# First-block scores of an attention kernel computed on array halves, with a rearranged opening

## The reference

```python
x = L0_attn_x                                  # (16, 256, 128), float32
xn = layernorm(x)
q = (xn @ Wq) ; k = (xn @ Wk)                  # 16 heads of 8
v = (xn @ Wv)                                  # 16 heads of 64
scores = einsum('bhqd,bhkd->bhqk', q, k) / sqrt(8)
scores = where(causal, -inf, scores)
ctx = einsum('bhqk,bhkd->bhqd', softmax(scores), v)
x = x + ctx.reshape(B, T, 1024) @ Wo
x = x + experts(layernorm(x), gate_w, w1, w2)  # softmax gate, top 64, gelu, scatter back
```

## Time and profile before

| | us |
|---|---|
| median of 3 runs (lowest to highest) | 560.72 (559.99 to 560.88) |
| the profiled execution | 560.4 |
| its span, first to last instruction | 558.7 |
| busy PE, DVE, ACT, POOL in that span | 527.9, 415.7, 403.8, 253.5 |

### The profile page before, as it was taken

How to read it: one execution, slowest core, us unless ns; L and a number is a source line. 1 busy time by engine, 2 the same in 40 slices (tenths; PEclk the granted TensorE clock), 3 DMA queues, 4 the chain that set the end, 5 groups by cost and what they waited for, 6 DMA issues and landing times.

```text
span 558.7 us, 13959 instructions
## 1 busy us (share of the span) xinstructions
PE 527.9 (94%) x4777; PEld 427.2 (76%) x4777; DVE 415.7 (74%) x1066; ACT 403.8 (72%) x1383; POOL 253.5 (45%) x249
## 2 busy tenths in 40 slices
PE   1389999999999999999999999999999999999996
PEld 1257777777777877877777777777789998999995
DVE  1477888888888888888898999899873776542354
ACT  4688888888888988989889888889745434334230
POOL 5165555555556556565565565556820101011011
PEclk9979999999999999999999999999999999999999
DMA  4585251732544225042250523410300011000011
GB/s 122 150 211 154 53 151 52 230 118 58 149 117 113 77 73 150 24 126 76 76 149 16 142 76 77 131 22 29 106 21 1 2 39 59 20 21 11 11 29 49
DMA packets 49783, 45.97 MB, mean 82 GB/s; under 512 B 4288, under 2 KB 46528, under 8 KB 49728
## 3 DMA queue, kind: packets, MB, share of 16 engines
q1 hardware_dynamic: 48864, 44.60, 29.2%
q10 hardware_dynamic: 864, 0.66, 0.4%
HBM read 26.35 MB, written 18.89 MB: 81 GB/s over the span
## 4 chain that ended last, share of the span: by engine, by line
PE 90%; ACT 4%; DVE 4%; issue 1%; DMA 1%; POOL 0%; ACTq 0%; DVEq 0%; POOLq 0%
PE ctx_ps L1075 16%; PE misc_ps L1084 12%; PE t_ps L1162 10%; PE t_ps L1048 6%; PE t_ps L1058 5%; PE t_ps L1049 5%; PE s_ps L1189 4%; PE misc_ps L1034 4%; PE s_ps L1146 4%; PE misc_ps L1036 3%; PE misc_ps L1035 3%; PE s_ps L1147 3%; PE s_ps L1148 3%; PE s_ps L1276 3%; PE ctx_ps L1172 2%; ACT prob L529 2%
## 5 line engine op out<-in xcount | busy, mean ns | idle before, releaser
L529 ACT ACTIVATE prob<-s_ps,neg_max 128x128 f32<-128x128 f32 (+1 forms) x512 | 209.9, 437 | 21.2 <-DVE neg_max L939 18.2
L489 POOL TENSOR_TENSOR probn<-prob,inv 128x1024 f32<-128x1024 f32 x64 | 121.2, 1893 | 56.3 <-DVE inv L960 56.3
L529 ACT ACTIVATION_READ_ACCUMULATOR prob<-s_ps,neg_max 128x1 f32 x512 | 114.5, 224 | 0.0
L482 POOL TENSOR_TENSOR probn<-prob,inv 128x512 f32<-128x512 f32 x64 | 66.5, 1040 | 77.7 <-PE t_ps L1058 69.6
L883 DVE TENSOR_REDUCE neg_max<-s_ps 128x4 f32<-128x1024 f32 x64 | 76.4, 1193 | 0.8 <-PE s_ps L1194 0.8
L1084 PE MATMUL misc_ps<-wo_sb,ctxT 128*128 128x128 f32 x512 | 73.9, 287 | 0.7 <-DVE x_all L708 0.7
L506 POOL TENSOR_TENSOR y_parts<-y_sb,y_parts 128x512 fp32r<-128x512 f32 x16 | 20.6, 1287 | 112.6 <-ACT y_parts L587 112.6
L1084 PEld LDWEIGHTS misc_ps<-wo_sb,ctxT 128*128 128x128 f32 x512 | 62.0, 191 | 11.4 <-issue 11.4
L577 ACT ACTIVATE hT<-s_ps 128x512 f32<-128x512 f32 x64 | 38.0, 597 | 44.7 <-PE s_ps L1148 42.2
L1048 PE MATMUL t_ps<-ident,probn 128*128 128x128 f32 x256 | 62.9, 285 | 0.5 <-ACT probT L543 0.5
L1049 PE MATMUL t_ps<-ident,probn 128*128 128x128 f32 x256 | 60.2, 275 | 0.0
(11 more groups left out here) (176 smaller groups left out, 1155.1 us busy)
## 6 DMA issues: line engine op xcount, KB each, us to landing
qT<-q_rows SPq DMA_DIRECT2D x15, 512.0 KB, 4.0
q_rows<-qk_hi SPq DMA_DIRECT2D x32, 128.0 KB, 2.4
q_rows<-qk_lo SPq DMA_DIRECT2D x32, 128.0 KB, 2.4
k_diag_odd<-k_rows SPq DMA_DIRECT2D x32, 128.0 KB, 4.2
k_rows<-qk_hi SPq DMA_DIRECT2D x30, 128.0 KB, 2.4
k_rows<-qk_lo SPq DMA_DIRECT2D x30, 128.0 KB, 2.4
k_diag_even<-k_rows SPq DMA_DIRECT2D x28, 128.0 KB, 4.2
w_raw<-in_L_ffn_w SPq DMA_DIRECT2D x1, 2048.0 KB, 9.5
```

The lines of the kernel that those rows point to most:

```text
L482: nc.gpsimd.tensor_tensor(probn[r][:, 0:HG * P].rearrange("p (i k) -> p i k", i=HG), prob[r][:, 0:HG * P].rearrange("p (i k) -> p i k", i=HG),
L489: nc.gpsimd.tensor_tensor(probn[r][:, HG * P:].rearrange("p (i k) -> p i k", i=HG), prob[r][:, HG * P:].rearrange("p (i k) -> p i k", i=HG ...
L529: last = nc.scalar.activation(prob[r][:, first + i * keys:first + (i + 1) * keys], scores[:, i, :], ACT.Exp, bias=neg_max[:, r, block_, i: ...
```

## The change

- First-block scores (`scores`) are two matmuls of 64 rows and 256 columns, `first_block(0)` on the lower and `first_block(1)` on the upper half of the array. Both write the one bank of `s0_ps`; a new semaphore `s0_half`, raised by `first_block(0)`, is waited for ahead of `first_block(1)`.
- First-block and second-block scores of a unit are issued together, at the end of slot u for unit u+2, in the order first(0), second(1), second(0), first(1), masks. The two halves of the array go through their two products in opposite orders. The wait for the exponentials of the unit before stands now between first(0) and second(1), ahead of `s0_done`.
- `turn(u-1)` comes first in PE's slot, ahead of queries and keys.
- DVE: the gate copy (L727) moves ahead of norms in slot 0; the second norm's statistics go behind the split of q and k in slot 3.
- Opening: the slots of b = -2 and -1 are replaced by a written-out sequence. DVE normalises batch 0 before it splits the weights of q and k. POOL makes both scales before the masks. Zeros of `k_diag` are made by ACT (two instructions) and DVE (six). ACT issues two of the first five loads. Second batch's norm, q and k, and values of units 0 and 1 come ahead of the scores of units 0 and 1.

The diff, cut to this:

```diff
@@ SP
                 if b < RING:
-                    sp.wait_ge(zeroed, b + 1)
+                    sp.wait_ge(zeroed, 3 + 4 * b)
                 if b == 0:
-                    load_rows(b, slice(0, 1), first_loaded)
+                    load_rows(b, slice(0, 1), first_loaded, range(2))
@@ POOL
+            norm1_scale(0)
+            norm1_scale(1)
+            masks()
...
@@ ACT
-            zero_keys(0)
...
+            split_norms(0, 0)
+            zero_keys(0, range(2))
+            split_qk(0)
+            act.wait_ge(qk_hi_done, 1)
+            store_rows(act, qk_hi, K_HI)
+            act.wait_ge(qk_lo_done, 1)
+            store_rows(act, qk_lo, K_LO)
+            act.wait_ge(wv_loaded, 16)
+            nc.scalar.activation(wv_hi[:, :], wv_raw[:, :], ACT.Copy).then_inc(w_hi, 1)
+            split_norms(1, 1)
+            act.wait_ge(qk_stored, QK_STORES)
+            act.wait_ge(zeroed, 3)
+            for i in range(2, HG):
+                act.dma_start(f32(k_diag[0][i * ROWS:(i + 1) * ROWS, 0:1, i, :]),
...
+            copy_values(0, 0, 0)
+            copy_values(1, 1, 0)
+            split_qk(1)
+            act.wait_ge(max0, 1)
+            exps(0, 0, s0_ps, P, 0, exp0)
+            act.wait_ge(max1, 1)
+            exps(0, 1, s1_ps, T, HG * P, exp1)
@@ DVE
+            norm_stats(lambda tb: x_all[:, tb, :], bn6, mv1, bn1_done, 1, stats1)
+            norm1(0)
+            split_qk_weights()
+            dve.wait_ge(x_loaded[1], 16)
+            norm_stats(lambda tb: x_all[:, TB + tb, :], bn6, mv1, bn1_done, 2, stats1)
+            split_norms(0, 0)
+            zero_keys(0, 2)
+            split_qk(0)
+            zero_keys(0, 3)
+            norm1(1)
+            zero_keys(1, 0)
+            dve.wait_ge(w_hi, 3)
+            nc.vector.tensor_tensor(wv_lo[:, :], wv_raw[:, :], f32(wv_hi[:, :]), ALU.subtract).then_inc(w_lo, 1)
+            split_norms(1, 1)
+            for j in range(1, G):
+                zero_keys(1, j)
+            dve.wait_ge(s0_done, 1)
...
@@ PE
+            def scores(w, q, kb):
+
+                tiles = ((slice(0, HALF), 0), (slice(HALF, P), 2))
+
+                def first_block(t):
+
+                    rows, i = tiles[t]
+                    return nc.tensor.matmul(s0_ps[:, i:i + 2, :], qT[kb][rows, q, 0:P], k_diag[kb][rows, q, i:i + 2, 0:P],
+                                            start=False, stop=True, skip_group_check=True)
+
+                def second_block(t):
+
+                    rows, i = tiles[t]
+                    nc.tensor.matmul(s1_ps[:, i:i + 2, :], qT[kb][rows, q, P:T], k_diag[kb][rows, q, i:i + 2, :],
+                                     start=True, stop=False, skip_group_check=True)
+
+                first_block(0).then_inc(s0_half, 1)
+                await_count(pe, exp1, w)
+                second_block(1)
+                second_block(0)
+                pe.wait_ge(s0_half, w + 2)
+                first_block(1).then_inc(s0_done, 1)
+                for half in range(2):
...
+                last.then_inc(s1_done, 1)
@@ PE, batch
-                    if has(u + 1, UNITS):
...
-                        last.then_inc(s1_done, 1)
+                    if has(u - 1, UNITS):
+                        turn(u - 1, rm)
...
-                        nc.tensor.matmul(s0_ps[:, :, :], qT[kb][:, q, 0:P], k_diag[kb][:, q, :, 0:P], start=False, stop=True,
-                                         skip_group_check=True).then_inc(s0_done, 1)
-
+                        scores(u + 2, (j + 2) % G, par if j < 2 else 1 - par)
@@ PE, opening
+            turn_first_norms(0)
...
+            queries_keys(0)
...
+            turn_first_norms(1)
...
+            values(0, 0)
+            pe.wait_ge(v_ready, 1)
+            values(1, 0)
+            pe.wait_ge(v_ready, 2)
+            queries_keys(1)
+            pe.wait_ge(first_loaded, QK_LOADS)
...
+            scores(0, 0, 0)
+            pe.wait_ge(qk_loaded, QK_LOADS)
+            pe.wait_ge(filled0, 1)
+            scores(1, 1, 0)
```

More of the change, by code:

```diff
@@ L229, in block_kernel @@
         v_ready = sem("v_ready")
+        s0_half = sem("s0_half")
         s0_done = sem("s0_done")
@@ L302, in batches @@
         def batches(engine, batch):
-            for b in range(-2, 4):
+            for b in range(4):
                 batch(b, b % 2)
@@ L465, in batch @@
                     if j == 1 and has(b + 2, B):
[L466 to L475, removed]
+                        norm1_scale(b + 2)
                     if j == 0 and has(b - 2, B):
@@ L915, in batch @@
                             copy_probs(0, misc_ps[0][0:HALF, T:2 * T])
+                    if j == 0 and has(b + 2, B):
+                        if isinstance(b, int) and b == 2:
+                            for i in range(2, len(XPARTS) - 1):
+                                dve.wait_ge(x_loaded[i], 16)
+                        norm_stats(lambda tb: x_all[:, (b + 2) * TB + tb, :], bn6, mv1, bn1_done, b + 3, stats1)
+                    if j == 1 and has(b + 2, B):
+                        norm1(b + 2)
+                    if j == 0 and has(b - 2, B):
+                        norm2(b - 2)
                     if j == 1 and has(b - 2, B):
@@ L1036, in split_product, with turn_first_norms, queries_keys @@
                 return nc.tensor.matmul(out_, w_l, x_h, start=False, stop=True)
+            def turn_first_norms(b):
+                pe.wait_ge(xn1_ready, b + 1)
+                for tb in range(TB):
+                    last = nc.tensor.transpose(misc_ps[0][:, tb * P:(tb + 1) * P], xn1[:, tb, :], ident[:, :])
+                last.then_inc(xT_done, 1)
+            def queries_keys(xb):
+                for w in range(2):
+                    last = split_product(misc_ps[0][:, w * T:(w + 1) * T], wqk_hi[:, w, :], wqk_lo[:, w, :],
+                                         xT_hi[xb][:, :], xT_lo[xb][:, :])
+                last.then_inc(qk_done, 1)
@@ new lines, in values @@
+            def values(q, xb):
+                toks = slice((q % 2) * P, (q % 2 + 1) * P)
+                cols = slice((q // 2) * 512, (q // 2 + 1) * 512)
+                split_product(misc_ps[0][:, :], xT_hi[xb][:, toks], xT_lo[xb][:, toks],
+                              wv_hi[:, cols], wv_lo[:, cols]).then_inc(v_done, 1)
+            def scores(w, q, kb):
[15 more added lines that the diff above has]
+                for half in range(2):
+                    cols = slice(P + half * HALF, P + (half + 1) * HALF)
+                    for rows, i in tiles:
+                        last = nc.tensor.matmul(s1_ps[:, i:i + 2, cols], half_rows[rows, half, :],
+                                                bcast(half_masks[rows, half, :], 1, 2),
+                                                start=False, stop=(half == 1), skip_group_check=True)
+                last.then_inc(s1_done, 1)
@@ L1221, in batch @@
                     if j == 2 and has(b + 2, B):
-                        pe.wait_ge(xn1_ready, b + 3)
                         await_count(pe, v_ready, u + 2)
-                        for tb in range(TB):
-                            last = nc.tensor.transpose(misc_ps[0][:, tb * P:(tb + 1) * P], xn1[:, tb, :], ident[:, :])
-                        last.then_inc(xT_done, 1)
+                        turn_first_norms(b + 2)
                     if has(u - 2, UNITS):
```

163 lines of the change are left out of this document (77 added, 86 removed).

## The result

The changed kernel takes 567.08 us median of 4 runs (567.02 to 567.28), the kernel before 560.80 (559.99 to 561.25): ratio 1.0116, 95% interval 1.0100 to 1.0132. The profiled execution took 567.1 us with a span of 565.3, so what lies around the span is 1.8 us (1.7 before). Forecast were 566.7 us, +6.0; measured +6.3.

The account below looks back on a forecast made before the run. PE, busy 328.27 of 329.00 us from 50 to 379, was taken as the bound. 558.7 + 5.9 + 0.4 + 0.0 - 0.3 = 564.7 us span; against the median 560.7 + 6.0 = 566.7 us, range 556.5 to 571.5.

Parts of the forecast that it names:

- block +5.9: PE's block of scores: each 0.10 us longer because of the wait on `s0_half`, over 59 blocks, +5.9 us.
- later scores at the end: Units 58 to 60: scores 0.52 us later reach PE because DVE has no idle time left; +0.4 us, bounds 0 and 1.5.
- ring in the opening: Units 1 to 4: exponentials, scores, maxima in a circle, exponentials of the unit before now ahead of `s0_done`; gives 0.2 us back.
- orders of PE and DVE: `turn` ahead of queries and keys, gate copy and statistics changing places within DVE's idle 13%: zero, bounds -0.5 and +0.5.
- opening without the ring: Written-out opening: exponentials of unit 0 at about 24.3 against 24.82, a gain of 0.5 us.
- the ring: Exponentials end, second(1) and first(1), maxima, next exponentials: put at 5.80 us, against a short PE slot of 5.80.
- Rival B: Block of scores: halves pay in full, first(0)'s result in time or weights loaded under the wait; 553.3 us (552 to 556), chance 0.14.
- rival C: Block of scores: only first(1)'s weights load ahead, wait on the matmul; -0.01 a block, 560 to 561.8 us, chance 0.12.
- `turn` moves past nothing that waits: PE's slot: the operands of `turn` are ready long before in the full stretch, so moving it costs zero.
- chain up to the first exponentials: Opening: loads, norms, weight splits, values, queries and keys, then scores of unit 0; exponentials at about 24.3, against 24.82.
- the clock rises earlier: Opening: reason for its bound of -1.5 us, as PE works from 16.5 on.
- Rival D: Steady slots: the circle of exponentials, scores and maxima becomes the bound; 573.5 us, chance 0.14, of which 0.08 above 571.5.

Follow-up runs that it names:

- opening and orders alone: Changed kernel without the scores' change: new opening and both orders kept, first block one full matmul, second block at next slot's head; 555.90 us, ratio 0.9921.
- doubled wait: Changed kernel with first(1) waiting for the result of second(0) instead of first(0); 583.46 us, ratio 1.0413.
- two other orders: Changed kernel with its half matmuls reordered, in two kernels: other half between, 574.45 us, and both halves first, 576.78 us.
- full block: Changed kernel with the first block again one 128-row, 512-column matmul without PE's own wait, opening and orders kept; 556.13 us, second time 556.29 us.
- full block behind exponentials: Kernel with the first block as one full matmul, the wait for exponentials moved ahead of it; 559.48 us, ratio 0.9985.
- `turn` first alone: Kernel before with only the transposes of the unit before moved ahead of queries and keys on PE, DVE unchanged; 559.33 us, ratio 0.9981.
- split block alone: Kernel before with only the scores as in the change, issued together at the slot's end; old opening and old orders; 577.68 us, ratio 1.0310.
- orders alone: Kernel before with PE's `turn` ahead of queries and keys and DVE's new order, nothing else; 557.74 us, ratio 0.9952.
- kernel without the wait: Changed kernel with first(1) writing into the second block's bank without a wait, leaving some scores out of `s0_ps`, for timing only; 555.34 us, ratio 0.9914.
- other half between: Changed kernel with the wait and first(1) put between second(1) and second(0); 574.45 us, ratio 1.0255.
- both halves first: Changed kernel with first(0), its wait and first(1) all ahead of the wait for exponentials; 576.78 us, ratio 1.0301.

## Why the prediction came out right, and where it was wrong

The time was right, and so was the price of the block, its largest term. That the sum came within a microsecond is luck: the later scores cost 4.7 us more than said, and the orders and the opening gave 2.7 and 1.3 us more than said.

| step | said | measured (medians, in us) |
|---|---|---|
| scores: block +5.9, later scores at the end +0.4, ring in the opening +0.2 | +6.5 | +11.2 (567.08 - 555.90) |
| orders of PE and DVE | 0.0 | -2.7 (557.74 - 560.42) |
| opening without the ring | -0.5 | -1.8 (555.90 - 557.74) |

- **The block, +0.10 us: right in each of its times.** Between units 5 and 58 the changed kernel loses 5.49 us to the kernel with opening and orders alone ((4.97 + 4.12) - (0.78 + 2.82)), 0.104 on average over 53 slots; 51 of them lose 0.08 to 0.13 and two, V of units 25 to 26 and 33 to 34, 0.27 and 0.29, whose cause wasn't looked for. first(1) starts 0.44 us behind first(0), made of the 0.28 us to a result, 0.05 to 0.06 of reaction (first(0)'s row ends at 258.95, first(1)'s weights begin at 259.01) and 0.11 of weights that load behind the wait. Rival B would have needed the wait to end in time; rival C is gone, as first(1)'s row of 0.38 us has the weights in it, where without the wait they are loaded ahead and it takes 0.28. The doubled wait and the two other orders show that each 0.11 us moved behind the wait is paid in full.
- **Later scores: the size was off, 0.6 said, some 5 measured.** The difference of 11.2 us less the block's steady part is in two places. Up to unit 5 it is 3.60 us (0.78 + 2.82). The first block standing behind the exponentials is part of it, as the kernel shows that does only this: 1.65 us against the second profile of the full block, 2.87 against the first. How the rest divides isn't shown. The second block right behind the first costs +0.70 by one profile of the full block (against opening and orders alone) and -0.52 by the other. And the halves' own price can't be read from their rows there: at unit 2 a 256-column matmul takes 0.58 us instead of 0.38, but the full block's matmul of 512 columns takes 0.79 instead of 0.40, as PE runs at the lower of its two rates in both. The changed kernel stays at it until 41.2 us, the full block behind exponentials until about 37.5, opening and orders alone until 36.0; from V of unit 3 to V of unit 4 they take 6.23, 4.80 and 4.95 us. I had seen the ring, and gave it 0.2 us, as exponentials that must end first anyway. They need not: with the first block ahead of the wait, its maxima run beside them. The second place is the end: behind unit 58 the changed kernel loses 2.4 us more ((6.6 + 4.9) - (4.97 + 4.12)), against 0.5 for five blocks. Its trace between V of units 60 and 61 (PE, DVE):

```profile
378.54 0.50 PE L1140 MATMUL s_ps<-k_diag_odd,qT 64*128 64x512 f32 x2 [0.16 <-ACT prob L553]
...
379.18 0.69 DVE L978 TENSOR_REDUCE neg_max<-s_ps 128x4 f32<-128x512 f32 x1 [0.33 <-PE s_ps L1134]
...
382.35 0.40 DVE L760 TENSOR_TENSOR x_all<-misc_ps,x_all 128x256 f32<-128x256 f32 x1
...
382.90 1.13 PE L1203 MATMUL misc_ps<-wo_sb,ctxT 128*128 128x128 f32 x8 [1.15 <-DVE x_all L760]
```

  V of unit 60 is 377.66, so the maxima start at V + 1.52; in the full block they start at V + 0.68 (369.43, V 368.75). The block itself makes 0.51 of these 0.84 us; the other 0.33 come from second(1), which waits there for the exponentials (first row). DVE has no gap up to its addition into `x_all`, which PE's projection waits for, so the 0.84 us come back as 7.11 instead of 6.25 us from V of unit 60 to V of unit 61. Units 58 and 62 lose 0.42 and 0.44. I had named this step, 0.4 us with the bounds 0 and 1.5; it was priced by the width of the shift without asking which PE step reads what DVE does behind the maxima.
- **The orders: 0.0 said, bounds -0.5 and +0.5, -2.7 measured.** I argued from the sum of DVE's idle time, 13%, and never looked for rows where PE waits for DVE in the kernel before. There was one: the values of unit 62 waited 0.78 us for the gate's copy (the kernel with `turn` first alone still shows the row), and a look at each slot's length shows it as 6.86 us where its like take 5.84. The split block alone shows how much both orders matter with the late scores: queries and keys wait there for `misc_ps`, and values for the gate's copy. My sentence that `turn` moves past nothing that waits was right and beside the point; it becomes the cover of what does.
- **The opening: -0.3 said with the ring, -1.8 without it.** The chain up to the first exponentials was about right, 24.3 said, 23.97 measured, from 24.82. What I left out: units 2 to 4 also profit. Unit 5's values come 2.2 us earlier with the new opening than with the orders alone (-2.82 against -0.65), beyond my bound of -1.5. My reason for that bound, that the clock rises earlier, did not come true in the changed kernel. The clock column can't tell it: it reads 1.00 from 20 to 40 us there, and the rate has to be read from the starts of the matmuls. Its 512-column matmuls of the values start 0.43 us apart at 37.67 and 38.10, where those at 384.54 and 384.77 are 0.23 apart, and the change comes in the transposes behind the scores of unit 3:

```profile
40.73 0.42 PE L1168 MATMUL t_ps<-ident,probn 128*128 128x128 f32 x1
40.95 0.42 PE L1167 MATMUL t_ps<-ident,probn 128*128 128x128 f32 x1
...
41.38 0.29 PE L1167 MATMUL t_ps<-ident,probn 128*128 128x128 f32 x1
41.50 0.27 PE L1168 MATMUL t_ps<-ident,probn 128*128 128x128 f32 x1
```

  So PE was at the lower of its two rates (1.2 and 2.4 GHz) up to 41.2 us. In the kernel before it was at the higher one from 25.3 to about 30.5, fell back after 1.68 us of idle time ahead of 32.15, and rose again at about 39.1. The gain of the opening is for the most part order and not clock: opening and orders alone has V of unit 2 at 28.77 and of unit 3 at 35.65, 1.0 and 1.7 us ahead of orders alone (29.75 and 37.38), though it ran at the lower rate all that time and the other at the higher one from 25.4 to about 30. Another 0.65 us come up to V of unit 4, where it is at the higher rate from 36.0 on and orders alone only from 39.2. One run against another differs by as much: in the last set the kernel before took 561.9 to 562.4 us in four of its 17 runs (granted clock 0.999 to 1.000), and 559.6 to 561.0 in the others (0.990 to 0.998); why wasn't looked into.
- **Rival D did not occur** in the steady stretch: short slots take 5.80 us, the block's own price, and the list of PE's waits from 50 to 366 us has none for L553. At unit 60 it does for once (the row at 378.54). I had put the ring at 5.80 us. The kernel without the wait has the same ring and slots of 5.59, so the ring is shorter than my estimate by at least 0.2 us.

Still open: the tail behind unit 63, where the first block behind the exponentials costs 0.8 us (2.24 to 3.0) and the changed kernel 0.5, was not followed to its rows.

## What to carry to other kernels

A matmul split onto halves of the array pays only if its parts need no order among themselves: with both halves in one PSUM bank, a result-to-start wait of 0.44 us took back more than the 0.12 us gained, and of the orders tried those that hid part of it put the first scores behind the exponentials. When a producer is moved behind a wait for its consumer's consumer, price it where the machine is not full, at the opening and the end, as well as in the steady slot. And read the lengths of all slots of a loop in the kernel before: one that is a microsecond longer than its like names a wait that a change of order can take away.

## What the runs showed of the hardware that was not expected

- Halves that need no order reach the full gain: 5.59 us a slot against 5.71, 0.12 us for 256 columns saved.
- A wait between two row tiles' matmuls costs 0.44 us from start to start, whether 512 columns, 1024 or none run between (258.57 to 259.01 in the changed kernel, 262.09 to 262.53 with the other half between, and one merged row of 0.82 us for two matmuls of 0.38 with both halves first).
- The clock column reads 1.00 in stretches where PE is at the lower rate from the start on: in the changed kernel from 20 to 40 us, with 0.43 us between matmuls of 512 columns instead of 0.23. In the kernel before it reads 0.83 there; PE had been at the higher rate and went back.
